# A short causal filter is moved from one engine to three, and two activation tables become one

## The reference

```python
x = jax.nn.sigmoid(ca_branch(avg) + ca_branch(mx)) * x
x = lax.conv_general_dilated(x, conv1d_w, (1,), [(DC - 1, 0)], ..., feature_group_count=DI)   # DC = 4, DI = 256
x = silu(x + conv1d_b[None, :, None])
x_dbl = jnp.einsum('ed,bdl->bel', x_proj_w, x)          # 8 + 16 + 16 rows
delta = jnp.einsum('dr,brl->bdl', dt_proj_w, dt_lo)
delta = jax.nn.softplus(delta + dt_proj_b[None, :, None])
# then a scan over the positions, with exp(delta * A) and delta * B * x
```

## Time and profile before

| what | us |
|---|---|
| three runs | 7225.46, 7226.98, 7230.36 |
| their median | 7226.98 |
| span of the profiled execution, first to last instruction | 7224.3 |
| `filter_and_steps`, first batch | about 5896 to 6021 |
| `scan`, first batch | about 6021 to 6370 |
| `filter_and_steps`, second batch | about 6416 to 6544 |

### The profile page before, as it was taken

The page is one execution under the profiler, slowest core; times in us unless marked ns, Lnnn a source line. Parts: engine busy times, 40 slices in busy tenths (PEclk is TensorE's granted clock), DMA queues, the critical chain, the costliest instruction groups (busy, mean ns, idle before and its releaser), DMA issues. The chain is left out here.

```text
span 7224.3 us, 96722 instructions
## 1 busy us (share of the span) xinstructions
PE 5188.5 (72%) x22750; PEld 3160.2 (44%) x22750; DVE 5418.1 (75%) x10550; ACT 4493.3 (62%) x11841; POOL 4825.0 (67%) x4571
## 2 busy tenths in 40 slices
PE   7767666666766667666666766776889957757758
PEld 7444444444444444344443443333544425635644
DVE  6777777777777777777777777773879989989961
ACT  4666666666666666666666666775346759959920
POOL 3777777777777777777777777771049946927900
PEclk9999999999999999999999998888999978978978
DMA  7887787878878788787887878885100011222335
GB/s 224 285 251 239 248 250 237 252 238 248 250 236 251 239 248 250 236 251 239 248 250 237 251 237 248 302 272 169 33 21 33 33 43 66 103 102 77 104 135 189
DMA packets 588994, 1413.05 MB, mean 196 GB/s; under 512 B 94548, under 2 KB 258657, under 8 KB 584033
## 3 DMA queue, kind: packets, MB, share of 16 engines
q0 software_dynamic: 308224, 1006.95, 45.4%
q1 hardware_dynamic: 278114, 397.66, 16.2%
q10 hardware_dynamic: 2304, 4.20, 0.2%
HBM read 1322.52 MB, written 85.86 MB: 195 GB/s over the span
## 5 line engine op out<-in xcount | busy, mean ns | idle before, releaser
L627 POOL DMA_INDIRECT st_corners<-corner_table,df_rows x3840 | 3638.4, 947 | 1263.2 <-issue 1048.0
L1000 ACT ACTIVATE st_corners<-st_corners,df_share 128x128 f32<-128x128 f32 x3840 | 1225.9, 390 | 1580.6 <-DMA st_corners<-corner_table,df_rows 1546.3
L900 PE MATMUL df_acc_ps<-df_turned,df_tapw 128*128 128x512 f32 x3840 | 1987.4, 643 | 39.7 <-DMA df_tapw<-in_tap_w_dram 36.4
L889 PE MATMUL df_turn_ps<-main_ident,df_sampled 128*128 128x128 f32 x3840 | 649.7, 295 | 1435.7 <-DVE df_sampled L673 1370.2
L889 PEld LDWEIGHTS df_turn_ps<-main_ident,df_sampled 128*128 128x128 f32 x3840 | 447.9, 149 | 2212.2 <-issue 2102.4
L668 DVE TENSOR_TENSOR st_corners<-st_corners,df_part_ps 128x512 f32<-128x512 f32 x960 | 660.3, 688 | 849.5 <-ACT df_part_ps L1000 837.7
L1000 ACT ACTIVATE df_part_ps<-st_corners,df_share 128x128 f32<-128x128 f32 x3840 | 1178.6, 351 | 30.6 <-DVE df_sampled L673 29.8
L173 PE MATMUL st_conv_ps<-st_ow,st_patch 128*128 128x147 f32 (+1 forms) x6272 | 989.8, 304 | 0.0
L900 PEld LDWEIGHTS df_acc_ps<-df_turned,df_tapw 128*128 128x128 f32 x3840 | 731.1, 208 | 571.8 <-issue 529.2
L173 PEld LDWEIGHTS st_conv_ps<-st_ow,st_patch 128*128 128x128 f32 x6272 | 892.8, 200 | 8.8 <-issue 8.1
L657 DVE TENSOR_TENSOR st_corners<-st_corners,df_weight_ps 128x512 f32<-128x512 f32 x960 | 657.9, 685 | 278.2 <-DMA st_corners<-corner_table,df_rows 272.9
(11 more groups left out here) (370 smaller groups left out, 5672.4 us busy)
## 6 DMA issues: line engine op xcount, KB each, us to landing
df_tapw<-in_tap_w_dram SPq DMA_DIRECT2D x962, 128.0 KB
sc_c_row<-c SPq DMA_DIRECT2D x128, 512.0 KB, 3.6
st_corners<-corner_table,df_rows POOLq DMA_INDIRECT x3840
y_b<-st_outs SPq DMA_DIRECT2D x128, 256.0 KB, 4.7
l1f_w<-in_w_dram SPq DMA_DIRECT2D x32, 1024.0 KB, 6.8
fu_spare<-y_b SPq DMA_DIRECT2D x64, 256.0 KB, 5.4
f_y_in<-y_b SPq DMA_DIRECT2D x64, 256.0 KB, 6.2
u<-dw_u SPq DMA_DIRECT2D x64, 256.0 KB, 2.1
```

What stands on the lines that cost most here:

```text
L627: nc.gpsimd.indirect_dma_start(corners[slot][:, j].rearrange("p v c -> p (v c)"), None, tables[g // GPB], bass.IndirectOffsetOnAxis(ap=row ...
L889: t = nc.tensor.transpose(turn_ps[pair][:, j * TILE:(j + 1) * TILE], sampled[pair][:, j, :], ident[:])
L900: m = nc.tensor.matmul(acc_ps[:, h, :], tapw[pair][:, h * P:(h + 1) * P], turned_sb[pair][:], start=first, stop=last, skip_group_check=not ...
L1000: nc.scalar.activation(dst, src, ACT.Copy, scale=share[slot][:, j - VT, v:v + 1]).then_inc(weighed_a, 1)
```

## The change

The filter is split over three engines.

- Half 0 goes to PE as products with diagonal matrices. ACT makes four 128x128 diagonals from the identity (`diag`). For each chunk, PE multiplies four of them with the input shifted by 0 to 3 positions and adds up in PSUM (`convolve(c)`), in the two PSUM tiles that later hold the transposes (`dut_ps`). ACT applies silu straight from PSUM, chunk by chunk (`active_pe`). Before `turn(0)` may write these tiles, all eight silus of half 0 must be done.
- Half 1 goes to DVE for part 0 and to POOL for parts 1, 2 and 3. POOL does each tap but the first as a multiplication into `scaled` and an addition in place, seven instructions of 128x1024 a part. They stand in POOL's queue ahead of `ss_du` of chunk 0.
- ACT loads one table set that has exponential and logarithm after `silu(0)`, and again after `silu(3)`, so that no load stands between them in the chunks.
- `widen(1)` moves up, ahead of `convolve(2)` to `convolve(7)`.

```diff
+            def convolve(c):
+                pe.wait_ge(u_loaded[c * SPAN // LP], 16 * HALVES)
+                if c >= 2:
+                    pe.wait_ge(active_pe, c - 1)
+                for k in range(CONV1):
+                    m = nc.tensor.matmul(conv_ps(c), diag[:, k, :], u[0][:, c * SPAN + k:c * SPAN + k + SPAN],
+                                         start=(k == 0), stop=(k == CONV1 - 1))
+                m.then_inc(filtered, 1)
...
             def project(c):
                 if c >= 1:
                     pe.wait_ge(kept, c)
-                pe.wait_ge(active, HALVES * (c * SPAN // LP + 1))
+                pe.wait_ge(active_pe, c + 1)
+                pe.wait_ge(active, c * SPAN // LP + 1)
...
+            pe.wait_ge(cleared, HALVES)
+            pe.wait_ge(diagonals, CONV1)
+            convolve(0)
+            convolve(1)
             project(0)
             widen(0)
             project(1)
+            widen(1)
+            for c in range(2, GPB):
+                convolve(c)
+            pe.wait_ge(active_pe, GPB)
             for c in range(GPB):
-                if c + 1 < GPB:
+                if 0 < c and c + 1 < GPB:
                     widen(c + 1)
...
+            for k in range(CONV1):
+                nc.scalar.activation(diag[:, k, :], ident[:], ACT.Copy,
+                                     scale=conv1_sb[:, 0, b, k:k + 1]).then_inc(diagonals, 1)
...
             def silu(q):
-                for h in range(HALVES):
-                    act.wait_ge(tapped, (q + 1) * CONV1 * HALVES - HALVES + h + 1)
-                    part = xs_sb[:, h, q * LP:(q + 1) * LP]
-                    nc.scalar.activation(part, part, ACT.Silu, bias=conv_b[:, h:h + 1]).then_inc(active, 1)
+                for c in range(q * LP // SPAN, (q + 1) * LP // SPAN):
+                    act.wait_ge(filtered, c + 1)
+                    nc.scalar.activation(xs_sb[:, 0, cols(c)], conv_ps(c), ACT.Silu,
+                                         bias=conv_b[:, 0:1]).then_inc(active_pe, 1)
+                if q == 0:
+                    act.wait_ge(tapped, CONV1)
+                else:
+                    act.wait_ge(tapped_pool, q * CONV1)
+                part = xs_sb[:, 1, q * LP:(q + 1) * LP]
+                nc.scalar.activation(part, part, ACT.Silu, bias=conv_b[:, 1:2]).then_inc(active, 1)
...
             silu(0)
+            nc.scalar.preload_act_table_set("natural_log_exp_and_others")
             keep_low(0)
...
             for q in range(1, PARTS):
                 silu(q)
+            nc.scalar.preload_act_table_set("natural_log_exp_and_others")
...
+            n = 0
+            for q in range(1, PARTS):
+                pool.wait_ge(u_loaded[q], 16 * HALVES)
+                dst = xs_sb[:, 1, q * LP:(q + 1) * LP]
+                for k in range(CONV1):
+                    src = u[1][:, q * LP + k:q * LP + k + LP]
+                    w = conv1_sb[:, 1, b, k:k + 1]
+                    if k == 0:
+                        nc.gpsimd.tensor_scalar(dst, src, w, None, ALU.mult).then_inc(tapped_pool, 1)
+                        continue
...
+                    nc.gpsimd.tensor_scalar(scaled[n % 2][:], src, w, None, ALU.mult).then_inc(scaled_done, 1)
+                    n += 1
+                    pool.wait_ge(scaled_done, n)
+                    pool.wait_ge(tapped_pool, (q - 1) * CONV1 + k)
+                    nc.gpsimd.tensor_tensor(dst, dst, scaled[(n - 1) % 2][:], ALU.add).then_inc(tapped_pool, 1)
```

More of the change, by code:

```diff
@@ L2187, in filter_and_steps @@
         du = [sb(f"du{s}", [P, HALVES, SPAN]) for s in range(2)]
+        diag = sb("diag", [P, CONV1, P])
+        scaled = [sb(f"scaled{s}", [P, LP]) for s in range(2)]
         low_ps = pb("low_ps", [P, SPAN])
@@ L2193, in filter_and_steps @@
         cleared = sem("cleared")
+        diagonals = sem("diagonals")
+        filtered = sem("filtered")
+        active_pe = sem("active_pe")
         tapped = sem("tapped")
+        tapped_pool = sem("tapped_pool")
+        scaled_done = sem("scaled_done")
         active = sem("active")
@@ L2214, in cols, with conv_ps @@
             return slice(c * SPAN, (c + 1) * SPAN)
+        def conv_ps(c):
+            return dut_ps[c % 2][:].rearrange("p j d -> p (j d)")
         @block.sync
@@ L2348, in _ @@
             dve.wait_ge(cleared, HALVES)
[L2349 to L2363, removed]
+            dve.wait_ge(u_loaded[0], 16 * HALVES)
+            dst = xs_sb[:, 1, 0:LP]
+            for k in range(CONV1):
+                src = u[1][:, k:k + LP]
+                w = conv1_sb[:, 1, b, k:k + 1]
+                if k == 0:
+                    v.tensor_scalar(dst, src, w, None, ALU.mult).then_inc(tapped, 1)
+                else:
+                    dve.wait_ge(tapped, k)
+                    v.scalar_tensor_tensor(out=dst, in0=src, scalar=w, in1=dst, op0=ALU.mult,
+                                           op1=ALU.add).then_inc(tapped, 1)
             for c in range(GPB):
@@ L2391, in _ @@
         def _(pool):
+            n = 0
+            for q in range(1, PARTS):
+                pool.wait_ge(u_loaded[q], 16 * HALVES)
+                dst = xs_sb[:, 1, q * LP:(q + 1) * LP]
+                for k in range(CONV1):
+                    src = u[1][:, q * LP + k:q * LP + k + LP]
+                    w = conv1_sb[:, 1, b, k:k + 1]
+                    if k == 0:
+                        nc.gpsimd.tensor_scalar(dst, src, w, None, ALU.mult).then_inc(tapped_pool, 1)
+                        continue
+                    if n >= 2:
+                        pool.wait_ge(tapped_pool, (n - 2) // (CONV1 - 1) * CONV1 + (n - 2) % (CONV1 - 1) + 2)
+                    nc.gpsimd.tensor_scalar(scaled[n % 2][:], src, w, None, ALU.mult).then_inc(scaled_done, 1)
[3 more added lines that the diff above has]
+                    nc.gpsimd.tensor_tensor(dst, dst, scaled[(n - 1) % 2][:], ALU.add).then_inc(tapped_pool, 1)
             for c in range(GPB):
```

## The result

| | before | after |
|---|---|---|
| median of five runs, us | 7227.51 (7225.46 to 7231.05) | 7253.47 (7252.36 to 7260.8) |
| span of the profiled execution | 7224.3 | 7250.5 |

The ratio is 1.0037, with a 95% interval of 1.0024 to 1.005. The change costs 26 us. The forecast was 7233, no measurable change, with a range to 7250. What happened is its fourth rival, "POOL decides, slower", and by more than that rival's 7245.

What follows compares the result with a forecast made beforehand. DVE's queue bounds the stage before chunk 2, with the ring DVE, POOL, PE, ACT close behind. Chunk 2 6.5 and 6.0 us later, less 2.6 and 3.6 behind it: +6.3 on 7224.3, 7230.6, median 7233; range 7212 to 7250.

Steps and rivals of the forecast that it cites:

- fourth rival: Before chunk 2: POOL multiplies at 2.39, filter ends at 5959.5, chunk 2 at 5968.7, 5.9 more per batch, 7245; chance 0.14.
- The skeleton: Filter to chunk 2: the latest of DVE's, PE's and POOL's chains sets chunk 2, at 5962.8, 6.5 us later than before.
- The head: Stage start to chunk 0: PE's first 16 records end at 5912.6, DVE begins chunk 0 at 5924.4, 12 us earlier.
- the second rival: PE keeps the upper clock level from 5908 on: 48 records end at 5946.5, chunk 2 at 5955.3, time 7213; chance 0.15.
- PE's chain: Before chunk 2: `widen(1)` ends at 5930.6, PE's 48 records at 5954.1, and chunk 2 starts at 5962.8.
- the price of POOL's one-input multiplication: In POOL's filter of half 1: 1.5 us each, between 0.9 and 2.39, so three parts end at 5946.1.
- the rival's own rule: Before chunk 2: POOL's multiplication decides from 2.1 us on; each 0.1 us beyond costs 2.4 us.
- The sum: Whole kernel: first batch +3.9, second +2.4, together +6.3 on 7224.3, 7230.6; the median 2.7 above the profiled span, 7233.
- Behind chunk 2: Six chunks from chunk 2 on: 57.2 us instead of 59.8 in the first batch, 3.6 less in the second.
- The tables: Table loads between exponential and logarithm go: behind chunk 2 2.6 us less in the first batch, 3.6 in the second.
- the ring's path: From chunk c to c+2 over DVE, POOL, PE, ACT, DVE: one table load goes per turn, two turns give 2.6 us.
- The range: Whole kernel: 7212 to 7250 us; chance 0.67 within 0.2% of before, 0.13 faster, 0.20 slower.

Runs made afterwards that it cites:

- half 1 on DVE: The kernel after with all four parts of half 1 filtered on DVE and none on POOL; 7226.77 us, ratio to before 0.9997.
- the joint table alone: The kernel before with only the two loads of the joint exponential and logarithm table set added; 7219.56 us, ratio to before 0.9987.
- part 3 only: The kernel after with POOL filtering only part 3 of half 1 and DVE parts 0 to 2; one run, 7229.2 us.
- with the two-input product: The kernel after with POOL's multiplications as two-input products, the weight spread by a stride of zero; 7236.65 us, ratio to before 1.001.
- two parts on PE: The kernel after with PE filtering parts 0 and 1 of half 0, DVE the rest, POOL none; 7201.36 us, ratio to before 0.9965.

## Why the prediction was wrong, point by point

- **The skeleton** was right: the start of chunk 2 sets the stage, and ACT's order (all silus ahead of `soften(2)`) makes it the later of PE's and POOL's chains. With half 1 on DVE it followed PE, and with POOL's multiplication shortened it followed POOL. The path behind each chain was put too short: for PE's it left out that `keep_low(2)` also waits for `turn(0)`, 1.2 us with half 1 on DVE, and behind POOL's last addition it had 9.2 where 11.0 passed.
- **The head.** Chunk 0 was forecast at 5924.4 and started at 5920.9. PE's first products ended at 5912.3 (5912.6 forecast) though the input came 1 us later. `project(0)` took 1.88 instead of the 3.60 that I carried over from the earlier trace rows, because PE was now granted 0.93 over 5912.4 to 5926. `widen(1)` ended at 5926.1, as the second rival had it (5925.9). It changes nothing, as DVE then waits.
- **PE's chain.** 48 records were to take 23.5 us and took 23.2, granted 0.50 until 5930 and 0.98 from there; they ended 4.8 earlier than forecast, because from `project(0)` to the first of them it took 11.8 (5926.06 - 5914.22) where 16.2 was forecast. From their end to DVE's chunk it is 9.5 where PE decides (half 1 on DVE), 8.7 forecast.
- **The step that failed is the price of POOL's one-input multiplication.** The prediction took 1.5 us, "from above the two-input product of this shape, 2.39". It measured 2.83 alone and 2.93 on average in this batch, above the supposed upper bound. A row for another operation with more operands isn't a bound; POOL takes longer for the instruction with fewer. POOL's first batch, by its terms: twelve multiplications 35.2 instead of 18, additions 21.1 instead of 21.5, dependent starts 0.8 in all instead of 1.8, start 2.4 later. It ended at 5964.1, 18.0 later than the forecast 5946.1. With 2.93, the rival's own rule (2.4 us for each 0.1 above 2.1) gives 7233 + 20 = 7253, which is the measured time. That it fits to the microsecond is luck: POOL began 1.5 us later against DVE's filter and the path behind it was 1.8 longer than the rule has them, while additions and starts were 1.6 shorter and the chunks behind chunk 2 1.8 and 1.1.
- **The rule of the Trainium skill** on the same instruction ("GPSIMD Engine Reference", Engine selection: one-input operations at roughly line rate, by its clock of 1.2 GHz an estimate of 0.85 us) is off by more than three times here; the measurement decides. The sum didn't rest on it.
- **Behind chunk 2** 57.2 and 58.7 were forecast, 55.4 and 57.6 measured.
- **The tables.** Behind chunk 2, 6.2 us was my sum for both batches. By the table it is 8.5 in the kernel before and 7.2 within the change. With what the loads give at chunk 2 itself they are worth 10.2 and 10.0. The direction was right, the size a little low. In the first batch, where two loads of 1.3 were to leave the ring's path, the six chunks are 3.0 shorter. That fits the trace's 1.28 and not the 2.66 of the Trainium skill ("ScalarE: Activation LUTs", What ACT_TABLE_LOAD costs), which would give 5.3. In the second they are 5.5 shorter, which alone doesn't tell the two apart. At the head of `scan` the load is gone and the exponential waits 2.24 us for its transfer: nothing, as forecast.
- **The range.** Its upper end, 7250, came from the same false bound, with the rival at 0.14. With a two-sided doubt on this one price, the rival's chance should have been about that of the forecast.

## What to carry to other kernels

Price an operation on an engine by a row of that operation on that engine, and where there is none, don't take a seemingly harder one as its upper bound: measure it first, or let the range go well past it. Taking work off the busiest engine pays only down to the point where its next wait ends on something else, so move as much as makes the chains meet: against the joint table alone, half of one half moved to PE gains 17 us (203.6 against 220.8), and all of the split as the change makes it loses 37. An engine that receives work must be looked at for what stands behind it in its queue: POOL's `ss_du` of chunk 0 waited 34 us behind the filter. Moving it ahead was not run. By the trace of after it could take at most some 2 us off chunk 2, an estimate: ACT, which does all silus first, would be ready for `keep_low(2)` at 5966.6 instead of 5968.8.

## What the runs showed of the hardware

- POOL's multiplication by a factor (128x1024, float32) takes 2.8 us with a factor per partition or a constant, an addition of two full operands 2.34, and a product with an operand of stride zero 1.90.
- DVE and POOL hold each other up. Two rows of after, POOL's multiplication and DVE's predicated copies in the same stretch:

```profile
5939.61 3.53 POOL L2439 TENSOR_SCALAR ss_scaled<-ss_u,l_conv 128x1024 f32<-128x1024 f32 x1
```

```profile
5939.83 2.13 DVE L2417 COPY_PREDICATED ss_poly<-ss_large,ss_ln 128x512 f32<-128x512 int32 x2
```

  The first is 2.83 when undisturbed, the second 1.30. DVE's comparisons just ahead took 3.66 instead of 0.75, its multiply-and-adds of the filter 4.66 instead of 3.93 with POOL beside them (part 3 only), while those of the polynomial, one of whose inputs lies in PSUM, kept their 4.87. The Trainium skill ("SBUF — State Buffer", Who interferes with whom) says that a DVE instruction with two SBUF inputs and a POOL instruction that reads SBUF shut each other out, and that one-input copies and multiplications on DVE do too when they run in a two-port mode. The traces agree for the predicated copies, whose mask and logarithm both lie in SBUF, for the filter, and for the polynomial, which has one SBUF input; that the comparisons ran in such a mode no run here shows. DVE waited for chunk 2 anyway, so this cost nothing in the end.
- PE was granted 0.98 of its clock through 19 us of uninterrupted records (5930 to 5949), its upper level of 2.4 GHz, and 0.50, the lower one of 1.2 GHz, in 5966 to 5976, after it had stood idle for 14.3 us waiting for POOL. There `turn(0)` took 1.97, where it had been 1.09, and `widen(2)` 3.77, as before. A wait so long isn't needed for that: with the two-input product PE waited 3.14 us ahead of `turn(0)`, and both took the same:

```profile
5970.81 1.97 PE L2288 MATMUL ss_dut_ps<-main_ident,ss_du 128*128 128x128 f32 x8 [3.14 <-POOL ss_du L2449]
5973.60 3.77 PE L2274 MATMUL ss_delta_ps<-ss_low,ss_dtproj 8*128 8x512 f32 x4 [0.82 <-ACT ss_low L2336]
```

  Where `turn(0)` followed without a wait (half 1 on DVE, part 3 only) it took 1.09, and `widen(2)` 2.69 and 1.98. With two parts on PE there were waits of 1.90 and 1.67 us, and the two took 1.09 and 3.65. So the slow `widen(2)` (3.65 to 3.77) goes with a wait of PE shortly ahead of it; no run changed such a wait by itself.
